# Attention kernel: blocks of two steps on TensorE, sums and Z in buffers of their own

## The reference

```python
xn = _layernorm(x, axis=-1)
# attention A: 8 heads, latent of 32, d_k 128 + 32 rotary dimensions
scores = einsum('bhsd,bhtd->bhst', q, k) * scale
attn = softmax(scores); o = einsum('bhst,bhtd->bhsd', attn, v_c)
# attention B: 16 heads of 16; tokens are put in two classes (pos / not pos) by a
# similarity, a query sees only the keys of its class and 5 register tokens
l = where(key_mask, logits, -inf); a = softmax(l)
out = x + attn_A(xn) + attn_B(xn)
```

## Time and profile before

| what | value |
|---|---|
| median of 3 runs | 3412.9 us (3410.66 to 3431.38) |
| profiled execution, its span | 3409.3 us |
| PE busy | 3051.9 us, 90% |
| DVE busy | 2265.2 us, 66% |
| ACT busy | 1709.1 us, 50% |
| POOL busy | 1060.2 us, 31% |
| DMA | 213.54 MB, mean 63 GB/s |

### The profile page before, as it was taken

One profiled execution on the slowest core, in us unless ns is written; L12 is line 12 of the kernel. 1 busy time (PEld: TensorE's weight loads), 2 busy tenths in 40 slices (PEclk: granted clock), 3 DMA queues, 4 the chain that ended last, 5 costly groups with the idle time before them and its releaser, 6 DMA issues.

```text
span 3409.3 us, 47004 instructions
## 1 busy us (share of the span) xinstructions
PE 3051.9 (90%) x17538; PEld 1327.5 (39%) x17538; DVE 2265.2 (66%) x4088; ACT 1709.1 (50%) x1948; POOL 1060.2 (31%) x552
## 2 busy tenths in 40 slices
PE   5538898999989998999989998999989999899997
PEld 4423433344333433344333433344333433344333
DVE  4435466776767667776767667776767667676782
ACT  1211354654555454654555454654555455654565
POOL 1021451235222451235222451235222451235201
PEclk8765999999999999999999999999989999999998
DMA  3212421450034201450034301450034201550001
GB/s 116 89 49 69 95 52 41 106 107 17 28 83 99 60 22 47 106 104 18 28 83 97 62 19 50 105 105 18 28 83 96 64 18 37 117 107 15 19 15 33
DMA packets 130051, 213.54 MB, mean 63 GB/s; under 512 B 48376, under 2 KB 76952, under 8 KB 129688
## 3 DMA queue, kind: packets, MB, share of 16 engines
q1 hardware_dynamic: 125480, 202.24, 24.9%
q10 hardware_dynamic: 4352, 8.39, 0.7%
HBM read 137.28 MB, written 73.02 MB: 62 GB/s over the span
## 4 chain that ended last, share of the span: by engine, by line
PE 75%; DVE 16%; issue 3%; DMA 3%; POOL 2%; ACT 1%; SPq 0%; DVEq 0%; POOLq 0%; ACTq 0%
PE O L1104 22%; PE M L1008 14%; DVE mx L1310 13%; PE M L1002 8%; PE S L1092 7%; PE S L1089 4%; PE M L1028 3%; PE M L1118 3%; PE M L1069 2%; PE M L974 2%; PE M L1037 2%; PE M L1071 2%; PE M L1024 1%; DMA kt_d<-stg 1%; PE M L1033 1%
## 5 line engine op out<-in xcount | busy, mean ns | idle before, releaser
L1310 DVE TENSOR_REDUCE mx<-M 128x1 f32<-128x512 f32 x3072 | 1975.6, 683 | 742.0 <-PE M L1008 443.8
L862 ACT ACTIVATE PT<-S 128x1024 f32<-128x1024 f32 x1280 | 1269.1, 1023 | 881.7 <-PE S L1092 572.9
L1008 PE MATMUL M<-KB,QB 50*128 50x512 f32 x2048 | 684.2, 488 | 129.4 <-DVE mx L1310 75.9
L1008 PEld LDWEIGHTS M<-KB,QB 50*128 50x128 f32 x2048 | 281.2, 189 | 796.2 <-issue 395.6
L1104 PE MATMUL O<-PT,VB 128*32 128x512 f32 x4096 | 562.9, 622 | 0.7 <-ACT PT L862 0.7
L1092 PE MATMUL S<-QB,KB 52*128 52x512 f32 x2048 | 527.1, 448 | 2.4 <-ACT PT L862 2.1
L1002 PE MATMUL M<-KA,QA 98*128 98x512 f32 x1024 | 449.8, 479 | 38.8 <-DVE mx L1310 15.5
L746 POOL TENSOR_TENSOR PT<-PT 128x2048 f32<-128x2048 f32 x64 | 292.2, 4566 | 381.9 <-PE O L1104 364.7
L862 ACT ACTIVATE PTx<-S 128x1024 f32<-128x1024 f32 x256 | 248.5, 1022 | 249.0 <-PE S L1089 248.9
L746 POOL TENSOR_TENSOR PTx<-PTx 128x2048 f32<-128x2048 f32 x64 | 292.2, 4566 | 228.8 <-PE O L1104 228.8
L1002 PEld LDWEIGHTS M<-KA,QA 98*128 98x128 f32 x1024 | 182.8, 195 | 352.6 <-issue 193.4
(11 more groups left out here) (146 smaller groups left out, 1940.0 us busy)
## 6 DMA issues: line engine op xcount, KB each, us to landing
qk_d<-stg SPq DMA_DIRECT2D x32, 1024.0 KB
KA<-kt_d SPq DMA_DIRECT2D x48, 512.0 KB, 7.3
QB<-qk_d SPq DMA_DIRECT2D x192, 128.0 KB
KB<-qk_d SPq DMA_DIRECT2D x192, 128.0 KB
kt_d<-stg SPq DMA_DIRECT2D x16, 1024.0 KB
RB<-recb_d SPq DMA_DIRECT2D x64, 256.0 KB
PT<-in_x SPq DMA_DIRECT2D x16, 512.0 KB, 3.8
xn_d<-xnT ACTq DMA_DIRECT2D x16, 512.0 KB, 2.8
```

The costliest lines, as they stand in the source:

```text
L862: nc.scalar.activation(probs(kind, of_a)[:, 2 * pair:2 * pair + 2, :], Sg[pair][:, :].rearrange("p (j s) -> p j s", j=2), ACT.Exp, scale=S ...
L1008: done = mm(m[:, :], QB[rows, 2 * q + a, at:at + P], KB[rows, 2 * q + a, keys], start=True, stop=True)
L1310: v.tensor_reduce(mx[:, g % 2, unit, kh:kh + 1], m[:, :], AX.X, ALU.max).then_inc(free, 1)
```

## The change

Steps are done in blocks of two (`RUN = 2`). On TensorE a block is: part 0, scores (step 1, pair 0), part 1, scores (step 1, pair 1), part 2, scores (step 2, pair 0), part 3, scores (step 2, pair 1), part 4, values, part 5, values, both of the block before, then in A the denominators of one pair of steps, part 6. The eight units of a block go as 2, 1, 1, 2, 2 into parts 0 to 4 (`SPREAD`), for every combination of A and B. Jobs go to part 2 (`MID`), after the unit there, and some move by a step or two; the second half of a fill now comes a block after the first. The `scores` of the second pair take their two row halves in the other order.

B steps now use `PT` and `PTx` in turn as A steps do, so that four steps' probabilities are held. POOL's sum goes to a new buffer `SUM` instead of in place, and waits for the denominators before it rather than for the values. `Z` gets a place of its own (it shared one with `PTx`) and is cleared once at the start, not in each batch; its load waits for the last reading of it. ScalarE follows the order of the block: fills are emptied between its four exponentials, `take_out` after the fourth. SP issues `shift` before `dens`. The scratch memory for dynamic DMAs is set to 1024 to make room.

```diff
+RUN = 2
+BLOCKS_A, BLOCKS_B = STEPS_A // RUN, STEPS_B // RUN
+GROUP = NC // RUN
+PARTS = 3 * RUN + 1
+SPREAD = ((0, 2), (2, 3), (3, 4), (4, 6), (6, 8))
+MID = 2
@@ place
-    for i in range(NC):
-        step, (u0, u1, u2, u3) = s[at + i], units[4 * i:4 * i + 4]
-        if kind == "b" and len(s) == STEPS_B:
-            step[0] += [u0, u1]
-            step[2] = [u2, u3] + step[2]
-        elif kind == "a" and len(s) == STEPS_A:
-            step[0] += [u0]
-            step[1] = [u1] + step[1] + [u2]
-            step[2] = step[2] + [u3]
-        else:
-            step[1] += [u0, u1]
-            step[2] = [u2, u3] + step[2]
+    for i in range(NC // RUN):
+        u = units[4 * RUN * i:4 * RUN * (i + 1)]
+        for part, (lo, hi) in enumerate(SPREAD):
+            s[at + i][part] = u[lo:hi] + s[at + i][part]
@@ jobs_b
-        for at, name in ((20, "kt0"), (24, "kb"), (28, "kt1"), (34, "qk0"), (42, "qk1"), (50, "qk2"), (58, "qk3")):
-            s[at][2].append((name, 0))
-            s[at + 1][2].append((name, 1))
+        for at, name in ((20, "kt0"), (24, "kb"), (28, "kt1"), (34, "qk0"), (40, "qk1"), (48, "qk2"), (58, "qk3")):
+            s[at // RUN][MID].append((name, 0))
+            s[(at + 2) // RUN][MID].append((name, 1))
...
-THREE = 3
+THREE = 2 // RUN
...
+    SUM = sb("SUM", [P, 4, HALF])
+    Z = sb("Z", [P, 2 * QB_ * 144], F32R)
@@ POOL
             k = 2 * i + 1
-            wait_apart(pool, pv_done, n * STEPS + k)
+            if n or i:
+                wait_apart(pool, dn_done, n * PAIRS + i)
             wait_apart(pool, e_done, n * (2 * STEPS) + (2 * k + 2))
-            to = probs("a", k - 1)
-            nc.gpsimd.tensor_tensor(to, to, probs("a", k), ALU.add).then_inc(summed, 1)
+            nc.gpsimd.tensor_tensor(SUM[:, :, :], probs(k - 1), probs(k), ALU.add).then_inc(summed, 1)
@@ TensorE, A (B alike)
-            for k in range(STEPS_A):
-                scores(n, k, "a", 0)
-                some(k, 0)
-                scores(n, k, "a", 1)
-                some(k, 1)
-                if k:
-                    values(n, k - 1, "a")
-                elif before:
-                    values(b, STEPS_B - 1, "b")
-                if k >= 3 and k % 2 == 1:
-                    denominators(n, b, (k - 3) // 2)
-                some(k, 2)
+            for d in range(BLOCKS_A):
+                for i in range(2 * RUN):
+                    some(d, i)
+                    scores(n, RUN * d + i // 2, "a", i % 2)
+                for i in range(RUN):
+                    some(d, 2 * RUN + i)
+                    if d:
+                        values(n, RUN * (d - 1) + i, "a")
+                    elif before:
+                        values(b, STEPS_B - RUN + i, "b")
+                if RUN * d >= 2 and RUN * (d + 1) % 2 == 0:
+                    denominators(n, b, RUN * (d + 1) // 2 - 2)
+                some(d, PARTS - 1)
```

More of the change, by code:

```diff
@@ L611, in a_steps @@
                     load_residual(b, 1)
+                kind, nxt = ("a", g + 1) if g + 1 < GA else ("b", 0)
+                shift(n, kind, nxt, a_spot(n, b, ("fa", kind, nxt)))
                 if g:
@@ L642, in b_steps @@
             for g in range(GB):
+                if g + 1 < GB:
+                    shift(b, "b", g + 1, b_spot(b, last, ("fa", "b", g + 1)))
+                elif not last:
+                    shift(n, "a", 0, b_spot(b, last, ("fa", "a", 0)))
                 if g:
@@ L646, in b_steps @@
                     dens(b, "a", GA - 1)
[L647 to L650, removed]
                 if g == 0:
@@ L843, in _, with exps @@
         nc.scalar.activation(root, n2, ACT.Sqrt).then_inc(root_out, 1)
-        def exps(n, k, kind):
+        def exps(n, k, kind, pair):
             step = n * STEPS + k
-            later = n > 0
-            of_a = k if kind == "a" else k - STEPS_A
-            if kind == "a" and of_a >= 4:
+            if pair == 0 and step >= 4:
                 act.wait_ge(pv_done, step - 3)
[L853 to L864, removed]
+                if 4 <= k < STEPS_A + 4:
+                    act.wait_ge(summed, n * PAIRS + ((k - 4) // 2 + 1))
+            act.wait_ge(s_full, n * (2 * STEPS) + (2 * k + pair + 1))
+            nc.scalar.activation(probs(k)[:, 2 * pair:2 * pair + 2, :],
+                                 Sg[pair][:, :].rearrange("p (j s) -> p j s", j=2), ACT.Exp,
+                                 scale=SCALE_A if kind == "a" else SCALE_B).then_inc(e_done, 1)
         def take_out(n, kind, g):
@@ L914, in b_steps @@
         def b_steps(b, last):
             slots = JOBS_LAST if last else JOBS_B
-            for k in range(STEPS_B):
-                exps(b, STEPS_A + k, "b")
-                if k == 0:
-                    take_out(b, "a", GA - 1)
[L920 to L927, removed]
-                fills(sum(slots[k], []), lambda j: b_spot(b, last, j), b + 1)
+            for d in range(BLOCKS_B):
+                if RUN * d == 2:
+                    take_dens(b, GA - 1)
+                fills(slots[d][0], lambda j: b_spot(b, last, j), b + 1)
+                for i in range(2 * RUN):
+                    exps(b, STEPS_A + RUN * d + i // 2, "b", i % 2)
+                    fills(slots[d][i + 1], lambda j: b_spot(b, last, j), b + 1)
+                    if i == 1 and RUN * d == 8:
+                        act.wait_ge(sr_ready, b + 1)
+                        nc.scalar.activation(SR[:, :], SR[:, :], ACT.Exp, bias=rmx[:, 1:2], scale=SCALE_B
+                                             ).then_inc(pr_ready, 1)
+                for i in range(RUN):
+                    fills(slots[d][2 * RUN + 1 + i], lambda j: b_spot(b, last, j), b + 1)
+                if d == 0:
+                    take_out(b, "a", GA - 1)
+                elif d % GROUP == 0:
+                    take_out(b, "b", d // GROUP - 1)
@@ L1085, in scores @@
                 pe.wait_ge(e_done, n * (2 * STEPS) + (2 * step + pair - 1))
-            for e in range(2):
+            for e in ((0, 1), (1, 0))[pair]:
                 to = Sg[pair][:, e * HALF:(e + 1) * HALF]
@@ L1103, in values @@
                 lhs = VA[:, c, :] if kind == "a" else of_v(c, 4 * q + jj)
-                last = mm(O[32 * jj:32 * jj + 32, :], lhs, probs(kind, k)[:, jj, :], start=(c == 0), stop=(c == NC - 1),
+                last = mm(O[32 * jj:32 * jj + 32, :], lhs, probs(step)[:, jj, :], start=(c == 0), stop=(c == NC - 1),
                           skip_group_check=True)
@@ L1175, in _ @@
         b_steps(B - 1, True)
-        values(B - 1, STEPS_B - 1, "b")
+        for i in range(RUN):
+            values(B - 1, STEPS_B - RUN + i, "b")
         for j in TAIL:
@@ L1386, in a_steps @@
             slots = JOBS_A if before else JOBS_A0
[L1387 to L1388 removed]
+            for d in range(BLOCKS_A):
+                for j in (j for part in slots[d] for j in part):
                     job(j, a_spot(n, b, j), b if j[0] == "po" else n, b)
[L1390 to L1392 removed]
+                if d % GROUP == GROUP - 1:
+                    if d >= GROUP:
+                        invert(n, "a", d // GROUP - 1)
                     elif before:
```

128 lines of the change are left out of this document (59 added, 69 removed).

## The result

| | before | changed |
|---|---|---|
| median | 3414.15 us (4 runs, 3410.66 to 3431.38) | 3678.32 us (4 runs, 3669.77 to 3688.64) |
| ratio | | 1.077, 95% interval 1.073 to 1.080 |
| profiled execution, span | 3409.3 us | 3667.9 us |
| mean granted TensorE clock | 0.945 | 0.906 |
| PE busy | 3051.9 us | 3305.8 us |

The change makes the kernel 7.7% slower. The prediction said slower, 3492 us with a range to 3560: the sign was right, the size a third of what came.

A forecast was written before the change was run, and what follows sets the result against it. The prediction took the PSUM banks' round trip through VectorE, plus the values group's hold on TensorE, to bound the plain step. Terms 19 + 13 + 54 + 0 + 7 + 0 - 14 = +79 us on 3409.3 gave 3488, median 3492, range 3395 to 3560.

The forecast's parts named there:

- What bounds the kernel: Plain B step: set by PSUM banks' round trip through VectorE and the values group's hold on TensorE, 2.93 us.
- B, maxima for B, plain: 192 B blocks taking maxima for B: 5.97 us a block against 5.87 for two steps, +19 us.
- A: A blocks, 64 of each kind: +0.2 each with maxima for A (+13 us), +0.85 with maxima for B (+54 us).
- upper schedule of the prediction: A block with maxima for B, score-to-maxima changes at the dearer 0.42 us: 8.46 us; the cheaper 0.33 gave 8.1.
- B, maxima for A: 56 B blocks taking maxima for A: 5.97 us a block against 5.98 for two steps, so nothing.
- The last groups: Last two groups of the last batch, 8 blocks without maxima: 4.9 us against 4.02, +0.9 each, +7 us.
- Jobs: Same job matmuls moved to mid-block: between -0.25 and +0.15 each for some 20 a batch, about zero, bounds ±25 us.
- The stall: ScalarE's 7.7 us wait for the kt0 store at the key fills: -2 for each of 7 batches, -14 us.
- The clock: Rival: TensorE's clock drops in a third of the 128 A blocks, about 3 us each, +130, 3620; chance 0.06.
- The rival of the saved switches: Saved values entries and exits count, 0.23 us in each of 384 blocks, 88 us: about 3315; chance 0.17.

The follow-up runs named there:

- longer reduction: Changed kernel with one more unused 0.60 us VectorE reduction ahead of that of the block's fifth maxima matmul, in all blocks with maxima for B: 3896 us, ratio 1.140.
- moved u1: Kernel before, with the second maxima matmul moved from before the second scores to behind them, in B steps taking maxima for B: 3365 us, ratio 0.982.

## Why the prediction was wrong

**What bounds the kernel.** Right: a plain step is the bank path, not TensorE's busy time. The longer reduction and the moved u1 both show it from the other side, to a few hundredths.

**B, maxima for B, plain.** Right: 5.97 forecast, 5.95 measured.

**A.** The sum was right, by luck, since the split was not. Forecast were 13 + 54 = 67 us, measured 70 at full clock. The plain block with maxima for B came at 8.47, the upper schedule of the prediction (8.46), of which I took 8.3. But with a `vb` job it takes 9.33, where two steps took 8.58, so that jobs give some back: 3.9 us a batch instead of 6.8. The blocks with maxima for A, all of which carry jobs in the middle batches, cost 4.8 us a batch, not 1.6.

**B, maxima for A.** A plain block takes 6.42, not 5.97, but over the two groups with their jobs before and after are equal (61.1 us for the same values). Right in the sum only.

**The last groups.** Right: 4.87 forecast as 4.9, as far as the clock holds (3612.75 to 3617.62).

```profile
3612.75 1.93 PE L1094 MATMUL O<-PT,VB 128*32 128x512 f32 x16
...
3617.62 3.60 PE L1094 MATMUL O<-PTx,VB 128*32 128x512 f32 x16
```

The second row is the next values pair, again at 1.2 GHz.

**Jobs.** The step "between -0.25 and +0.15, about zero" failed. In B groups 0 to 5 they make most of the 10.9 us a batch: two-matmul fills 0.77 against 0.59, four-matmul fills 1.64 against 1.30 (and the output projections likewise), `rs` 4.9 against 4.2, `va` 4.9 against 3.1. I had worked out +0.15 for a fill, over its own block alone, and left out that before it removed the step's bank wait. Up to 80 us of the miss. About 30 of them are shown at full clock (fills, projections and `rs`, 4 us a batch). The rest stands at the six places without a sample at full clock: the `va` block's 4.9 has a granted clock of 0.81, and with blocks in B alone the same block costs 3.8 at 0.91, so most of what `va` seems to lose is the clock's.

**The stall.** Forecast -14 us. The wait itself fell from 51.9 to 43.2 us in all. The interval at kb holds 5.3 us over its neighbour instead of 8.1, but that of its second half 1.4 more: about -10, all three at a granted clock of 0.77 to 0.88. Right in sign and near in size.

**The clock.** The step that failed worst. I had it as a rival at 0.06, with falls in a third of the A blocks. It is at least 100 us, and sits at the end of A and in the first half of the B blocks, where the trace of before had the falls behind `rv` and `lat` and at the kb stall. The rival expected it in A; it is mostly in B. That plain steps run at 1.00 was taken as evidence that plain blocks would, though the block puts all values together and leaves 4.1 us between in which eight pairs of matmuls at 0.24 stream, less than half of it. What in this brings the falls about stays open.

**The rival of the saved switches** is out. The entry and exit are saved (two groups and the way back take 1.86 on the rows above), and paid for by the bank. It decided at 5.8 for a plain block, and that is 5.95.

Of +258, 157 are in the shortest intervals (70 in A, 87 in B, some of the latter the clock's) and about 100 beyond them at the clock. The forecast +79 were 67 in A, 19 in B, -14 and 7. What is missing is up to 80 in the B jobs and at least 100 at the clock. The range was wrong in its sum as well, though not so as to matter: its bounds, added up, give 3392 to 3542 and not 3420 to 3550, and none of them has the clock.

## What to carry to other kernels

Where an engine hands results on through few banks, write the step as one path over the bank that is free last, and look at what stands between that hand-over and the next long block of other work. Moving one matmul out of that path gave 1.8%; gathering the other work into longer blocks, to save ways in and out, lengthened it and, with the falls of the clock, cost 7.7%. And price a job by what it hides in its old place, not by its own length.

## What the runs showed of the hardware

TensorE's granted clock fell to 1.2 GHz in a plain block without a stall: 7.9 us for 5.9 us of work, with TensorE busy for 96% of them by the profile's modelled ends (7.59 of 7.90). With two matmuls of 0.24 us repeated in each B block it stayed at 2.4 GHz there in all six middle batches, where it had fallen in five, and the kernel became 1.2 to 1.6% faster; a third round did nothing more. But with no more matmuls, after a change in A blocks alone, it stayed up there in four of six. In the order of single steps one more matmul a step brought the clock nothing. What exactly makes it fall stays open. The Trainium skill (TensorE: Matmul & The Clock Gate, "A second HAM failure mode: psum-queue depth-cycling") names a kernel whose clock goes back and forth since TensorE idles for moments between groups while it cycles through PSUM banks. The clock of 0.74 in the block with bank waits agrees, though a block with the same waits ran at 1.00 (1893.80 above); that the number of matmuls in the waits decides it, no run here shows beyond the three above.
